# Reordering VectorE's work in the layer-1 attention: the residual update between the two halves of the softmax, and the mean square before the modulation

## The chip, the cores and the metric

The kernel runs on one core of a Trainium2 chip. The metric is the device time of one execution in microseconds (us). Most executions agree within about 0.3%. Everything is float32. The profile shown is of one execution, taken by the hardware profiler; times in it count from its first instruction.

Names of the engines: TensorE (PE, with its weight loads as PEld), VectorE (DVE), ScalarE (ACT), GpSimd (POOL), SyncE (SP). Each runs its own list of instructions strictly in the order in which it was written. They meet only at semaphores: an instruction waits until a counter has reached a number, and raises a counter when it is done.

## The reference, cut to what matters

128 sequences of 32 tokens with 128 features pass through two transformer blocks. Both are conditioned on one vector per sequence. The change is in the attention of the second one (layer 1), which has a single head of width 128:

```
x_in = x
h = rmsnorm(x, norm1_w) * (1 + scale) + shift          # scale, shift from cond
Q, K, V = h @ q_w + q_b, h @ k_w + k_b, h @ v_w + v_b
attn = softmax((Q @ K.T) * D ** -0.5, axis=-1)         # 32 keys for each token
x = x_in + (attn @ V) @ proj_w + proj_b
# behind it the second MLP:
x = x + gelu(film(rmsnorm(x, norm2_w)) @ mlp_w1 + mlp_b1) @ mlp_w2 + mlp_b2
```

## The kernel before, in words

The 4096 rows are 32 tiles of 128 rows (four sequences each), and four tiles are a group: there are 8 groups (`NG = 8`). All of `X` stays in SBUF. The kernel has four phases, each over all 8 groups: layer-0 attention, layer-0 MLP, layer-1 attention (`attention1`), layer-1 MLP (`mlp(3)`). A group's norm is prepared under a running number `gg = phase * 8 + g`, and this preparation runs ahead of the phase by two or three groups. There is no scheduler: every engine's order is written out by hand as a step function, and `group_steps` calls it for g = 0 to 7. Buffers are doubled; `p` is the half.

In step g of the layer-1 attention each engine does this, in this order:

- **TensorE**: `qkv1(g)`: Q and K into banks 2 and 3, then V (with the output projection already folded into its weights, `wvp`) into bank 4. The V part waits until VectorE has copied the previous group's V out of bank 4 (`v1_moved >= g`). Then `rows_T(g+2)` transposes the normed rows `xhat` of the group two ahead into `hT_ps` (bank 0); it waits for `xhat_ready`. Then `scores1(g)` into bank 7, which waits for ScalarE's copies of Q and K of this group. Then, for g of at least 2, `values1(g-2)`: attention weights `PT` times values `Vs`, into `y_ps` (bank 1). It waits for `pt1_ready`, `v1_moved` and for the update of group g-3, which empties the same bank.
- **ScalarE**: the exponential of group g-1 (`exps1`, `St<-Ss`), which waits for VectorE's subtraction of that group; two square sums of group g+3; the copies of Q and K of group g (`Qs`, `Kx`); two more square sums.
- **GpSimd**: `power1` (`rstd<-v_sb`) and `scale_rows` (`xhat<-X,rstd`) of group g+3, then `add_shift` (`h<-hA,B`) of group g+2, then `keep` (`xg<-X,row`, X plus the projection's bias) of group g.
- **VectorE**: `softmax1(g-1)`: row maximum and subtraction from bank 7 into `Ss`. `normalise1(g-1)`: the sum of the exponentials (`den`), its reciprocal (`rden`), the product `St<-St,rden`, and a transposition into `PT`. It waits for the exponential. `move_v1(g)` copies V from bank 4 to `Vs[p]`; that half of `Vs` is still read by `values1(g-2)`, so the copy waits for `y_ready`, which `values1(g-2)` raises. `modulate(g+2)` (`hA<-bank,A`). `mean_square(g+3)` (`v_sb<-ssq`), for which GpSimd's `power1` waits. `update(2, g-2)` (`X<-bank,xg`), which also needs the `y_ready` of `values1(g-2)`.

The lines which the prediction names: L539 and L541 maximum and subtraction; L547, L549, L551, L556 the four of `normalise1`; L563 V's copy; L481 `modulate`; L569 `mean_square`; L494 `update`; L388 and L381 GpSimd's `power1` and `scale_rows`; L332 `keep`; L308 `add_shift`; L879 the exponential; L895 and L897 the copies of Q and K; L887 the squares; L924 `rows_T`; L1094, L1095 and L1098 Q, K and V; L1108 `scores1`; L1121 `values1`; L949 the first matrix of the MLP (`up`); L1087 its second (`down`); L757 ScalarE's `xhat` of the MLP phase; L468 a part of VectorE's `aggregate`.

At the start of `mlp(3)` TensorE does `up` of group 0, chunks 0 and 1 (banks 2 and 3), `values1(6)`, chunks 2 and 3 (banks 4 and 5), `rows_T`, `values1(7)`; VectorE does `softmax1(7)`, `normalise1(7)`, `update(2,6)`, row statistics, `modulate`, `aggregate`.

Of the kernel before, what the change touches and what calls it, by code (L numbers as in the profile page):

```python
# [31 lines left out]
NG = NT // TG  # L32
# [26 lines left out]
def build(nc, x, cond, weights, columns, rows, out):  # L59
    with ExitStack() as ctx:  # L60
# [3 lines left out]
        def sem(name):  # L64
            return ctx.enter_context(nc.semaphore(name))
# [73 lines left out]
        qkv1_ready, qk1_moved, v1_moved, s1_ready, max1_ready, s1_used, p1_ready, den1_ready, rden1_ready, p1_scaled, pt1_ready, ssq_ready = (  # L139
            sem(n) for n in ("qkv1_ready", "qk1_moved", "v1_moved", "s1_ready", "max1_ready", "s1_used", "p1_ready", "den1_ready",  # L140
                             "rden1_ready", "p1_scaled", "pt1_ready", "ssq_ready"))
# [5 lines left out]
        def w(name, i=0, n=D):  # L147
            at = W_AT[name][0] + i * n
            return W[:, at:at + n]
# [8 lines left out]
        def by_tile(ap):  # L158
            return ap.rearrange("p (t d) -> p t d", t=TG)

        def by_seq(ap):
            return ap.rearrange("p (b t) -> p b t", t=L)

        def over_keys(ap):
            return ap.unsqueeze(2).broadcast_to([P, TG, L])

        def wait(eng, s, n):

            if not isinstance(n, int) or n > 0:
                eng.wait_ge(s, n)  # L170
# [11 lines left out]
        def known(g, low, high):  # L182

            return not isinstance(g, int) or low <= g < high

        def x_group(gg):

            if isinstance(gg, int):
                g = gg % NG
                return slice(g * TG, (g + 1) * TG)  # L190
            return bass.ds(((gg) % NG) * TG, TG)
# [236 lines left out]
        def _(dve):  # L428
# [46 lines left out]
            def modulate(gg, p, stats_of=None):  # L475

                if stats_of is not None:
                    dve.wait_ge(stats_done, stats_of + 1)
                dve.wait_ge(hT_ready, gg + 1)
                wait(dve, h_ready, gg - 1)  # L480
                dve.tensor_tensor(by_seq(hA[:, p, :]), by_seq(hT_ps[:, :]),  # L481
                                  A[:, seqs(gg)].unsqueeze(2).broadcast_to([P, GB, L]), ALU.mult).then_inc(hA_ready, 1)

            def update(phase, g, p):

                gg = phase * NG + g
                dve.wait_ge(y_ready, gg + 1)
                if phase < 2:
                    dve.wait_ge(x_updated, gg + 1)
                    dve.tensor_tensor(by_tile(yG[:, :]), by_tile(y_ps[:, :]), gate[:, phase, x_group(g), :],  # L490
                                      ALU.mult).then_inc(y_used, 1)
                else:
                    dve.wait_ge(xg_ready, gg + 1)
                    dve.tensor_tensor(X[:, x_group(g), :], by_tile(y_ps[:, :]), by_tile(xg[:, p, :]),  # L494
                                      ALU.add).then_inc(x_updated, 1)
# [40 lines left out]
            def softmax1(g, p):  # L536

                dve.wait_ge(s1_ready, g + 1)
                dve.tensor_reduce(max1[:, :], by_seq(bank[7][:, 0:P]), AX_X, ALU.max).then_inc(max1_ready, 1)  # L539
                dve.wait_ge(max1_ready, g + 1)  # L540
                dve.tensor_tensor(by_seq(Ss[:, p, 0:P]), by_seq(bank[7][:, 0:P]), over_keys(max1[:, :]),  # L541
                                  ALU.subtract).then_inc(s1_used, 1)

            def normalise1(g, p):

                dve.wait_ge(p1_ready, g + 1)
                dve.tensor_reduce(den1[:, :], by_seq(St[:, p, 0:P]), AX_X, ALU.add).then_inc(den1_ready, 1)  # L547
                dve.wait_ge(den1_ready, g + 1)
                dve.reciprocal(rden1[:, :], den1[:, :]).then_inc(rden1_ready, 1)  # L549
                dve.wait_ge(rden1_ready, g + 1)  # L550
                dve.tensor_tensor(by_seq(St[:, p, P:2 * P]), by_seq(St[:, p, 0:P]), over_keys(rden1[:, :]),  # L551
                                  ALU.mult).then_inc(p1_scaled, 1)
                dve.wait_ge(p1_scaled, g + 1)
                if known(g, 2, NG):
                    dve.wait_ge(y_ready, 2 * NG + g - 1)
                dve.transpose(PT[:, p, 0:P], St[:, p, P:2 * P]).then_inc(pt1_ready, 1)  # L556

            def move_v1(g, p):

                dve.wait_ge(qkv1_ready, 3 * g + 3)  # L560
                if known(g, 2, NG):
                    dve.wait_ge(y_ready, 2 * NG + g - 1)
                dve.tensor_copy(Vs[:, p, 0:GN], bank[4][:, :]).then_inc(v1_moved, 1)  # L563

            def mean_square(gg, p):

                dve.wait_ge(ssq_ready, gg - 2 * NG - 2)
                wait(dve, rstd_ready, gg - 1)
                dve.tensor_scalar(v_sb[:, p, :], ssq[:, p, :], 1.0 / D, 1e-6, ALU.mult, ALU.add).then_inc(v_ready, 1)  # L569
# [141 lines left out]
            def attention1(g, p):  # L711
                first = isinstance(g, int) and g == 0
                if not first:
                    softmax1(g - 1, 1 - p)
                    normalise1(g - 1, 1 - p)
                move_v1(g, p)
                if first:
                    mean_square(2 * NG + g + 3, 1 - p)
                    update(1, 7, 1)
                modulate(2 * NG + g + 2, p)  # L720
                if not first:
                    mean_square(2 * NG + g + 3, 1 - p)
                if known(g, 2, NG):
                    update(2, g - 2, p)

            group_steps(dve, attention0)
            group_steps(dve, mlp(1))
# [186 lines left out]
        def _(pe):  # L914
# [28 lines left out]
            def up(phase, g, p, chunks=range(NC)):  # L943

                m = (phase // 2) * NG + g
                pe.wait_ge(h_ready, phase * NG + g + 1)
                for n in chunks:
                    wait(pe, g_ready, NC * (m - 1) + n + 1)
                    last = pe.matmul(bank[2 + n][:, :], w(f"W1_{phase // 2}", n), h[:, p, :], start=True, stop=True)  # L949
                    last.then_inc(u_ready, 1)  # L950
# [46 lines left out]
            def output_T(g, p):  # L997

                pe.wait_ge(o_used, 2 * g + 2)
                pe.wait_ge(y_used, g + 1)  # L1000
                for t in range(TG):
                    last = pe.transpose(bank[1][:, P * t:P * (t + 1)], On[:, p, P * t:P * (t + 1)], ident[:, :])
                last.then_inc(ot_ready, 1)
# [108 lines left out]
            def wait_values1(g):  # L1112
                pe.wait_ge(pt1_ready, g + 1)
                pe.wait_ge(v1_moved, g + 1)
                pe.wait_ge(x_updated, 2 * NG + g + 1)

            def values1(p):
                for t in range(TG):
                    for b in range(TB):
                        rows_of = slice(L * b, L * (b + 1))  # L1120
                        last = pe.matmul(y_ps[rows_of, P * t:P * (t + 1)], PT[rows_of, p, L * t:L * (t + 1)],  # L1121
                                         Vs[rows_of, p, P * t:P * (t + 1)], start=True, stop=True)
                last.then_inc(y_ready, 1)

            def mlp(phase):
                def step(g, p):
                    gg = phase * NG + g
                    first = isinstance(g, int) and g == 0
                    if first and phase == 1:
                        output_T(7, 1)  # L1130
                    elif first:
                        up(phase, g, p, (0, 1))
                        wait_values1(6)
                        values1(0)
                        up(phase, g, p, (2, 3))
                    elif not (phase == 1 and isinstance(g, int) and g == 1):
                        up(phase, g, p)
                    if first and phase == 1:
                        up(1, 1, 1, (0, 1))
                        project0(7, 1)  # L1140
                        up(1, 1, 1, (2, 3))
                    if phase < 3 or not isinstance(g, int) or g < 6:
                        rows_T(gg + 2, p)
                    if not first:
                        down(phase, g - 1, 1 - p)
                    elif phase == 3:
                        wait_values1(7)
                        values1(1)
                return step
# [64 lines left out]
```

## Time and profile before

| | |
|---|---|
| time, median of 3 runs | 293.84 us (293.37 to 294.67) |
| the profiled execution's own time | 293.45 us |
| its span, first to last instruction | 291.6 us |
| mean granted TensorE clock | 0.988 of full speed |
| busy: PE, DVE, ACT, POOL | 251.1, 187.1, 165.3, 184.6 us |
| layer-1 attention, first Q matmul to last step's start of `mlp(3)` | about 177.4 to 226.3 us |

The span is 1.85 us shorter than the execution's own time. The busy times are sums over four phases with different limits, so what the change is worth has to be read in the layer-1 attention itself: about 49 us in which one step follows another at an even pace.

### The profile page before, as it was taken

What the parts mean: (1) busy time and instruction counts of PE and PEld (TensorE: products, weight loads), DVE (VectorE), ACT (ScalarE), POOL (GpSimd) and SP (SyncE); (2) the same over time, 40 slices, a digit from 0 to 9 for tenths busy, and PEclk for the clock granted to TensorE, in tenths of its full rate; (3) what the DMA queues carried; (4) which work ended last, traced back from release to release, by engine and by line L of the source; (5) the groups of instructions that cost most, each with busy time, mean ns of one, the idle gap of its engine ahead of it and who ended that gap; (6) DMA issues with size and microseconds to landing.
All of it is one profiled execution on the core that took longest, in us unless ns stands there. A gap on an engine that the chain in (4) does not pass through costs nothing.

```text
span 291.6 us, 8250 instructions
## 1 busy us (share of the span) xinstructions
PE 251.1 (86%) x2876; PEld 188.1 (64%) x2876; DVE 187.1 (64%) x535; ACT 165.3 (57%) x358; POOL 184.6 (63%) x187
## 2 busy tenths in 40 slices
PE   0687739797989979889999999987678989999996
PEld 0565529586787767567777778655455567777775
DVE  4898974988999989855455554665654855452002
ACT  2265755686797875785555556434554555555330
POOL 5645375647678677579787888676777654445310
PEclk9999996999999999999999999999999999999999
DMA  7952769424434338800000000000000001111112
GB/s 227 328 176 37 168 111 197 71 62 70 82 75 76 74 71 167 182 4 0 1 0 0 0 0 2 0 2 1 0 2 0 0 4 36 36 36 36 38 36 72
DMA packets 44569, 18.11 MB, mean 62 GB/s; under 512 B 32512, under 2 KB 43136, under 8 KB 44032
## 3 DMA queue, kind: packets, MB, share of 16 engines
q1 hardware_dynamic: 43968, 15.80, 24.6%
q10 hardware_dynamic: 576, 1.98, 2.0%
q8 instruction: 15, 0.25, 0.4%
q14 instruction: 10, 0.08, 0.1%
HBM read 11.35 MB, written 4.59 MB: 55 GB/s over the span
## 4 chain that ended last, share of the span: by engine, by line
PE 53%; DVE 12%; DMA 9%; ACT 9%; issue 8%; POOL 4%; SPq 1%; DVEq 1%; ACTq 1%; POOLq 0%
PE bank L1087 20%; PE bank L949 16%; PE bank L979 5%; DMA values_scratch<-Vs 5%; PE bank L924 4%; ACT Kx L772 4%; DMA Vx<-values_scratch 3%; PE bank L1121 3%; PE bank L992 2%; DMA X<-x 2%; DVE hA L481 2%; ACT xhat L757 2%; SPq L239 1%; PE bank L1008 1%; DVE X L494 1%
## 5 line engine op out<-in xcount | busy, mean ns | idle before, releaser
L757 ACT ACTIVATE xhat<-X,shift,rstd 128x128 f32 (+1 forms) x96 | 39.6, 486 | 53.3 <-POOL shift L297 53.1
L1087 PE MATMUL bank<-W,Qx 128*128 128x128 f32 x512 | 59.6, 275 | 0.0
L1087 PEld LDWEIGHTS bank<-W,Qx 128*128 128x128 f32 x512 | 58.5, 192 | 1.0 <-issue 1.0
L949 PE MATMUL bank<-h,W 128*128 128x512 f32 x128 | 58.6, 596 | 0.0
L308 POOL TENSOR_TENSOR h<-hA,B 128x512 f32<-128x512 f32 x32 | 33.9, 1060 | 23.1 <-DVE hA L481 22.8
L807 ACT ACTIVATE Qx<-bank,col 128x512 f32<-128x512 f32 x64 | 39.2, 679 | 8.6 <-PE bank L949 8.6
L481 DVE TENSOR_TENSOR hA<-bank,A 128x512 f32<-128x512 f32 x32 | 22.0, 689 | 32.7 <-PE bank L924 17.3
L979 PE MATMUL bank<-Kx,Qx 128*128 128x128 f32 x256 | 36.2, 286 | 4.6 <-DMA Qx<-Qs 1.6
L949 PEld LDWEIGHTS bank<-h,W 128*128 128x128 f32 x128 | 22.8, 190 | 22.4 <-issue 22.1
L979 PEld LDWEIGHTS bank<-Kx,Qx 128*128 128x128 f32 x256 | 31.8, 196 | 6.6 <-DMA Qx<-Qs 1.8
L339 POOL TENSOR_TENSOR X<-yG,xg 128x512 f32 (+1 forms) x16 | 20.4, 1275 | 18.6 <-DVE yG L490 18.5
L295 POOL TENSOR_TENSOR rstd<-v_sb,minus_half 128x4 f32<-128x4 f32 x24 | 24.5, 1019 | 11.2 <-DVE v_sb L472 6.7
L924 PE MATMUL bank<-ident,xhat 128*128 128x128 f32 x128 | 20.6, 284 | 12.3 <-POOL xhat L381 7.1
L924 PEld LDWEIGHTS bank<-ident,xhat 128*128 128x128 f32 x128 | 14.8, 143 | 22.6 <-issue 13.7
L772 ACT ACTIVATE Kx<-bank,k_bias,r_mask 128x512 f32<-128x512 f32 x32 | 23.1, 777 | 9.7 <-PE bank L960 9.7
L315 POOL TENSOR_TENSOR Ss<-Sc,smax 128x512 f32<-128x512 f32 x16 | 16.8, 1049 | 17.7 <-DVE smax L505 17.6
L992 PEld LDWEIGHTS bank<-Vx,PT 128*32 128x32 f32 x1024 | 11.4, 112 | 21.9 <-issue 12.6
L332 POOL TENSOR_TENSOR xg<-X,row 128x512 f32<-128x512 f32 x16 | 20.3, 1269 | 7.1 <-DVE X L494 7.0
L789 ACT ACTIVATE PT<-St 128x512 f32<-128x512 f32 x32 | 20.3, 635 | 7.5 <-DVE St L518 7.5
L494 DVE TENSOR_TENSOR X<-bank,xg 128x512 f32 (+1 forms) x15 | 10.3, 686 | 19.8 <-PE bank L1087 19.8
L518 DVE STREAM_TRANSPOSE St<-Ss 128x512 f32<-128x512 f32 x32 | 21.9, 683 | 1.0 <-POOL Ss L315 0.9
L452 DVE BATCH_NORM_STATS2 stats<-X 128x6 f32 (+1 forms) x96 | 20.6, 278 | 2.7 <-DMA X<-x 2.2
(123 smaller groups left out, 414.9 us busy)
## 6 DMA issues: line engine op xcount, KB each, us to landing
values_scratch<-Vs SPq DMA_DIRECT2D x8, 288.0 KB, 2.5
Vx<-values_scratch SPq DMA_DIRECT2D x32, 72.0 KB, 2.6
gate<-gates_scratch SPq DMA_DIRECT2D x8, 256.0 KB, 4.8
gate<-gates_scratch SPq DMA_DIRECT2D x4, 512.0 KB, 7.6
Qx<-Qs SPq DMA_DIRECT2D x28, 64.0 KB, 2.3
out<-X SPq DMA_DIRECT2D x7, 256.0 KB, 2.3
W<-weights ACTq DMA_DIRECT2D x1, 1152.0 KB, 6.8
X<-x SPq DMA_DIRECT2D x4, 256.0 KB, 7.0
```

Of the source, the lines that this page charges most:

```text
L295: pool.tensor_tensor(rstd[:, p, :], v_sb[:, p, :], minus_half[:, :], ALU.pow).then_inc(pool_chain, 1)
L308: pool.tensor_tensor(by_seq(h[:, p, :]), by_seq(hA[:, p, :]), B[:, seqs(gg)].unsqueeze(2).broadcast_to([P, GB, L]), ALU.add).then_inc(h_re ...
L452: last = dve.bn_stats(stats[:, t, :], X[:, x_tile(gg, t), :])
L481: dve.tensor_tensor(by_seq(hA[:, p, :]), by_seq(hT_ps[:, :]), A[:, seqs(gg)].unsqueeze(2).broadcast_to([P, GB, L]), ALU.mult).then_inc(hA_ ...
L518: dve.transpose(St[:, t % 2, :], Ss[:, t % 2, :]).then_inc(st_ready, 1)
L757: last = act.activation(xhat[:, p, P * t:P * (t + 1)], X[:, x_tile(gg, t), :], ACT.Identity, bias=shift[:, p, t:t + 1], scale=rstd[:, p, t ...
L772: last = act.activation(Kx[:, p, q, :], bank[3][:, :], ACT.Identity, bias=k_bias[:, q:q + 1], scale=r_mask[:, q:q + 1])
L807: act.activation(gT[:, p, n, :], bank[2 + n][:, :], ACT.Gelu, bias=bias).then_inc(g_ready, 1)
L924: last = pe.transpose(hT_ps[:, P * t:P * (t + 1)], xhat[:, p, P * t:P * (t + 1)], ident[:, :])
L949: last = pe.matmul(bank[2 + n][:, :], w(f"W1_{phase // 2}", n), h[:, p, :], start=True, stop=True)
L979: last = pe.matmul(bank[4 + t % 2][:, P * b:P * (b + 1)], Qx[:, p, TB * t + b, :, :].rearrange("p a t -> p (a t)"), Kx[:, p, :, at:at + L] ...
L1087: last = pe.matmul(y[t // 2][:, P * t:P * (t + 1)], gT[:, p, n, P * t:P * (t + 1)], w(f"W2_{phase // 2}", n), start=(n == 0), stop=(n == N ...
```

## The change

VectorE's step of the layer-1 attention gets another order. Before: maximum and subtraction of g-1; the rest of the softmax of g-1; V's copy of g; modulation of g+2; mean square of g+3; update of g-2. After: maximum and subtraction of g-1; update of g-2; the rest of the softmax of g-1; V's copy of g; mean square of g+3; modulation of g+2. In step 0 nothing changes (V's copy, mean square, update of the layer-0 MLP's last group, modulation). In step 1 there is no update, and only the mean square and the modulation change places. No instruction on VectorE is added or removed.

On TensorE one wait is added: before the first `up` of the layer-1 MLP it waits until V of all 8 groups has been copied (`v1_moved >= 8`). Before, the wait for the update of group 5 ahead of `values1(6)` covered this, because the update stood behind V's copy in VectorE's order.

```diff
@@ VectorE, attention1(g, p) @@
                 first = isinstance(g, int) and g == 0
                 if not first:
                     softmax1(g - 1, 1 - p)
+                if known(g, 2, NG):
+                    update(2, g - 2, p)
+                if not first:
                     normalise1(g - 1, 1 - p)
                 move_v1(g, p)
+                mean_square(2 * NG + g + 3, 1 - p)
                 if first:
-                    mean_square(2 * NG + g + 3, 1 - p)
                     update(1, 7, 1)
                 modulate(2 * NG + g + 2, p)
-                if not first:
-                    mean_square(2 * NG + g + 3, 1 - p)
-                if known(g, 2, NG):
-                    update(2, g - 2, p)
@@ TensorE, mlp(phase) @@
                     if first and phase == 1:
                         output_T(7, 1)
                     elif first:
+                        pe.wait_ge(v1_moved, NG)
                         up(phase, g, p, (0, 1))
                         wait_values1(6)
                         values1(0)
```

## Rows read from the trace of the kernel before

**Rows 1.** The page, its first line.

```profile
span 291.6 us, 8250 instructions
```

**Rows 2.** Busy time by engine of one step (start:end, length, then each engine's).

```profile
201.20:207.50 6.30, 4.97 (x81) 3.35 (x82) 3.82 (x11) 2.74 (x11) 4.34 (x4) 1.00 0.00 0
```

**Rows 3.** Chain of waits that ended last, two pieces of one step (start, length).

```profile
208.86 0.59 DVE X L494
...
211.56 0.68 ACT Kx L897
```

**Rows 4.** Timeline of one step: start, length, engine, line, [idle before <- releaser].

```profile
207.49 0.69 DVE L563 COPY Vs<-bank 128x512 f32<-128x512 f32 x1 [1.84 <-PE bank L1121]
208.10 0.68 DVE L481 TENSOR_TENSOR hA<-bank,A 128x512 f32<-128x512 f32 x1
...
208.70 0.16 DVE L569 TENSOR_SCALAR v_sb<-ssq 128x4 f32<-128x4 f32 x1
...
208.77 0.68 DVE L494 TENSOR_TENSOR X<-bank,xg 128x512 f32 x1
208.94 1.02 POOL L388 TENSOR_TENSOR rstd<-v_sb,minus_half 128x4 f32<-128x4 f32 x1 [1.59 <-DVE v_sb L569]
...
209.68 0.29 DVE L541 TENSOR_TENSOR Ss<-bank,max 128x128 f32<-128x128 f32 x1
...
210.08 0.31 ACT L879 ACTIVATE St<-Ss 128x128 f32<-128x128 f32 x1 [3.59 <-DVE Ss L541]
...
211.28 0.65 PE L924 MATMUL bank<-ident,xhat 128*128 128x128 f32 x4 [1.05 <-POOL xhat L381]
...
212.24 1.26 POOL L332 TENSOR_TENSOR xg<-X,row 128x512 f32<-128x512 f32 x1
...
212.28 0.46 PE L1108 MATMUL bank<-Kx,Qs 128*32 128x32 f32 x32 [0.35 <-ACT Kx L897]
...
213.82 0.69 DVE L563 COPY Vs<-bank 128x512 f32<-128x512 f32 x1 [2.10 <-PE bank L1121]
```

**Rows 5.** Timeline of VectorE, the rest of the softmax of group 7.

```profile
229.25 0.29 DVE L547 TENSOR_REDUCE den<-St 128x4 f32<-128x128 f32 x1 [0.38 <-ACT St L879]
229.57 0.18 DVE L549 RECIPROCAL rden<-den 128x4 f32<-128x4 f32 x1
229.79 0.33 DVE L551 TENSOR_TENSOR St<-St,rden 128x128 f32<-128x128 f32 x1
230.16 0.31 DVE L556 STREAM_TRANSPOSE PT<-St 128x128 f32<-128x128 f32 x1
230.39 0.65 DVE L494 TENSOR_TENSOR X<-bank,xg 128x512 f32<-128x512 f32 x1
```

**Rows 6.** Timeline of step 1 to 2, VectorE beside GpSimd.

```profile
189.31 0.90 DVE L569 TENSOR_SCALAR v_sb<-ssq 128x4 f32<-128x4 f32 x1
...
191.63 1.04 POOL L381 TENSOR_TENSOR xhat<-X,rstd 128x512 f32<-128x512 f32 x1 [0.24 <-POOL rstd L388]
191.64 1.18 DVE L551 TENSOR_TENSOR St<-St,rden 128x128 f32<-128x128 f32 x1
```

**Rows 7.** Timeline, V's copies of step 2 and step 7 (the first and last of six).

```profile
194.91 0.69 DVE L563 COPY Vs<-bank 128x512 f32<-128x512 f32 x1 [1.66 <-PE bank L1121]
...
226.39 0.69 DVE L563 COPY Vs<-bank 128x512 f32<-128x512 f32 x1 [2.10 <-PE bank L1121]
```

**Rows 8.** Timeline of TensorE at the start of the layer-1 MLP.

```profile
226.26 1.99 PE L949 MATMUL bank<-h,W 128*128 128x512 f32 x4
...
228.50 1.08 PE L1121 MATMUL bank<-Vs,PT 32*32 32x128 f32 x32 [0.26 <-DVE X L494]
...
237.32 0.65 PE L924 MATMUL bank<-ident,xhat 128*128 128x128 f32 x4 [0.76 <-ACT xhat L757]
```

**Rows 9.** TensorE's clock: timeline, one window (clock third from last), longest waits after 51 us.

```profile
43.32 0.71 PE L992 MATMUL bank<-Vx,PT 128*32 128x36 f32 x32 [3.90 <-DMA Vx<-values_scratch]
...
42.00:43.00 1.00, 0.00 (x0) 0.00 (x0) 0.95 (x3) 0.00 (x0) 1.00 (x2) 0.71 0.73 116
...
PE bank L992 <- DMA Vx<-values_scratch: 3.8, 4, 1.6
```

## The prediction

> **What bounds the kernel now.** I read the page first: the span is 291.6 us [rows 1], and the profiled execution took 293.45 us, so 1.85 us lie around the span. That execution is 0.39 us under the median of the runs, 293.84 us. TensorE is the busiest engine, but the question is the layer-1 attention alone. So I read a table of busy time by stretch there: in one step of 6.30 us TensorE has 4.97 us of work, GpSimd 4.34, VectorE 3.82, ScalarE 2.74 [rows 2]. No engine is full. The pace must come from a loop through several of them.
>
> The chain of waits names the loop. In every step it goes through VectorE's update and through ScalarE's copy of K [rows 3]. The timeline of one step gives its lengths [rows 4]. I measure from the moment at which `values1` is seen to be done, which is the start of V's copy (207.49):
>
> - V's copy to modulation 0.61, to mean square 0.60, to update 0.07, to subtraction 0.91 (209.68, with the maximum in between), to the exponential 0.40 (210.08). Sum 2.59.
> - From the exponential to the scores, through squares, Q's copy and K's copy: 212.28 less 210.08, 2.20. TensorE stood idle for the last 0.35 of it because of K's copy.
> - From the scores to the next V copy, through `values1`: 213.82 less 212.28, 1.54.
>
> 2.59 + 2.20 + 1.54 = 6.33, one step. Over five steps the V copies go from 194.91 to 226.39 [rows 7], which is 6.30 each. A second loop is almost as long: mean square (208.70), GpSimd's power and `xhat`, the transposition of rows at 211.28, 2.58 later. TensorE waited 1.05 for it, but the scores behind it waited another 0.35 for K's copy. So the second loop has 0.35 us to spare.
>
> The reader should see what is **not** in the loop: the rest of the softmax. Its four instructions run while `values1` is still to come, and then VectorE stands idle for 1.84 to 2.10 us before V's copy [rows 4]. Today that part costs nothing, and this idle time is its cover.
>
> **The change part by part.**
>
> *Update before the rest of the softmax.* The update of g-2 needs `values1(g-2)`, the last thing in TensorE's step g. VectorE executes in order, so everything behind the update now starts after `values1` is done: the rest of the softmax, V's copy, mean square, modulation and, in the next step, the maximum and the subtraction for which the exponential waits. The cover is gone. The idle time moves ahead of the update, where nothing fills it. The price is what lies between the start of the sum `den` and the instruction behind the transposition. Row by row it is 0.32 + 0.22 + 0.37 + 0.23: 230.39 less 229.25 is 1.14 [rows 5]. The other members of the chain are the same as before in another order, so they add nothing. The new first loop is 6.30 + 1.13 = 7.43: I start from the mean step and take 1.13, since the product's own length varies by some hundredths.
>
> *Mean square before modulation.* This takes 0.60 out of the second loop, but the update (0.60) and the rest of the softmax (1.14) come in ahead of the mean square, where V's copy (0.61) stays and the modulation (0.60) leaves. Mean square starts at 0.60 + 1.14 + 0.60 = 2.34 after `values1`, where it was at 1.21. The rows' transposition starts 2.58 later, at 4.92, and ends at 5.57. The scores can go when K's copy is there: at 2.59 + 1.14 + 2.20 = 5.93. So the first loop stays in front, by 0.36, and the move is worth nothing. Below nothing is excluded for a reason: no instruction of the first loop goes away.
>
> *V's copy* comes at 1.74 and ends at 2.43 (0.69 long). TensorE's V matmuls for the next group need bank 4. They come after Q and K, which take about 2.1, so they start some 0.3 late. That is inside the time in which TensorE waits for `xhat` anyway (until 4.92), and costs nothing.
>
> *How often.* The update stands in steps 2 to 7. The loop is closed from step 2's `values1` to step 7's: five turns, 5 x 1.13 = 5.65. Step 1 has only the exchange of mean square and modulation. There the mean square took 0.90 instead of 0.16 [rows 6], so moving it ahead may give or cost some tenths; I take a gain of 0.1.
>
> *The start of the MLP.* Before, TensorE began `up` at 226.26, or 0.13 before V's copy of step 7, and then idled 0.26 until the update of group 5 let `values1(6)` go [rows 8]. Now it waits for V's copy of step 7, which ends at 2.43, so `up` starts at about 2.5, 2.63 later than before. The 0.26 of idle time falls away because the update is long done. Net 2.63 - 0.26 = 2.37. Nothing later gives it back: the next wait of TensorE, 0.76 at 237.32 for ScalarE's `xhat` [rows 8], follows from the rows' transposition that stands behind these same matmuls, and so moves with them. The bounds here are 0.9 (were the copy seen 1.14 earlier and hidden partly behind the exponential) and 3.0.
>
> *The product beside GpSimd.* It was 0.33 in one row and 1.18 in another, which began 0.01 after GpSimd's `xhat` and ended just behind it [rows 5, 6]. These are the two bounds of this instruction. In the new order GpSimd's step ends with `keep` (212.24 to 213.50), 0.3 before the next `values1` is seen, and GpSimd then waits for a mean square that comes at 2.34. The product runs at about 1.15 to 1.5. So I take 0.33. The Trainium skill has a rule for this, in "SBUF — State Buffer", section "SBUF: two separate sides": VectorE with two SBUF inputs and GpSimd share a port pair that one of them locks for a whole instruction. By that rule too the product is free here, since GpSimd is idle; the sum by the rule is the same unless GpSimd runs late, which is a rival below.
>
> **Sum**: 5.65 - 0.1 + 2.37 = 7.92. 293.45 + 7.9 = 301.4 for a profiled execution, and 293.84 + 7.9 = **301.7** for the median. This is 2.7% slower. What a measurement of this kernel can tell from no change is about 0.5%, or 1.5 us.
>
> **Rivals.**
>
> 1. *The rest of the softmax stays hidden* (not slower). If it did not delay the subtraction, the first loop would remain 6.33, and the second would be 0.60 + 0.60 + 2.58, then 0.65 for the rows, then 1.54: 5.97, shorter. Only the MLP's start would pay: V's copy ends at 1.29, `up` starts 1.5 later than before, less 0.26: +1.2, or 295.0, within 0.5%. For it speaks that exponentials are ready early in the new order, so `den` itself waits for nobody. Against it: it decides itself by whether `values1(g-2)` is done when VectorE reaches the update, and VectorE reaches it after the subtraction, at some 3.7 in a step of 7.4. It would have to be 3.7 us earlier. 3%.
> 2. *A collision with GpSimd in every step.* `keep` ends only about 0.3 before the update starts. If GpSimd's instructions move by more than 1.2 us against VectorE's, the product is blocked and takes up to 1.18: 0.85 more in each of five steps, 4.2, so 306. Against it: GpSimd's 4.34 of work fits into 7.4. 5%.
> 3. *TensorE's clock falls.* It was granted half speed (1.2 of 2.4 GHz) for some microseconds after TensorE had been idle for 3.90 us; within that idle time the clock went to 0.71 for the window 42 to 43. Later waits of up to 1.6 us left it at full speed [rows 9]. Now TensorE idles up to 1.3 us in a step, and about 2.5 at the start of the MLP, between the two. One step at half speed would be 2 x 4.97 = 9.9 of TensorE's work [rows 2] instead of a step of 7.4: 2.5 more, 304.2. 8%.
> 4. *A smaller price*: the MLP absorbs part of its late start (0.9 instead of 2.37), giving 300.2. 10%.
> 5. *It turns out faster* by something I don't see, such as the early update freeing `y_ps`: nobody waits for that bank within the phase. At best 0.35 of loop slack times five, 292.1. 3%.
>
> **How the numbers follow.** The forecast has 71%, with 300.6 to 302.8 of its own. The range 299.6 to 304.6 takes in rivals 4 and 3; outside are 1, 2 and 5 and the rest. Slower by over 0.5%: forecast, 2, 3 and 4, 94%. Within 0.5%: 3%. Faster: 3%.
>
> **What would show it.** In the profile after: V's copies of steps 2 to 7 some 7.4 us apart, with no idle time before them. VectorE's long idle time stands before the update instead, ended by `values1`, and is about 3.8 us (a step of 7.43, less 3.33 to the subtraction and its own 0.29). `den` has no wait for the exponential. TensorE waits some 1.3 for `xhat` and 0.3 for K's copy in each step. `up` starts behind V's copy with about 2.5 us of idle time. It would be wrong if the steps were still 6.3 apart (rival 1), if the product took over 1 us (rival 2), or if the clock in the stage were below 1 (rival 3).

## The result and the profile after

The changed kernel took 305.23 us (median of 4 runs, 303.55 to 306.81), the kernel before 294.25 us (4 runs). The ratio is 1.0365, with a 95% interval of 1.0317 to 1.0413. The forecast was 301.7 us with a range of 299.6 to 304.6. The direction was right and the added time was 11 us instead of 7.9, outside the range.

The page after, its span and the granted clock of TensorE in 40 slices (tenths of full speed; each slice is 7.6 us):

```profile
span 303.8 us, 8256 instructions
...
PEclk9999988799999999999999999997899799999999
```

The clock now falls twice more, in slices 28 and 29 and in slice 32 (counted from 1), which is the layer-1 attention and the start of the MLP behind it. Before, it stayed at full speed from 51 us on.

The timeline of one step in which the clock was at 1, the columns as in [rows 4]:

```profile
195.21 0.69 DVE L494 TENSOR_TENSOR X<-bank,xg 128x512 f32 x1 [4.71 <-POOL xg L332]
...
195.81 0.28 DVE L547 TENSOR_REDUCE den<-St 128x4 f32<-128x128 f32 x1
...
196.12 0.18 DVE L549 RECIPROCAL rden<-den 128x4 f32<-128x4 f32 x1
...
196.34 0.29 DVE L551 TENSOR_TENSOR St<-St,rden 128x128 f32<-128x128 f32 x1
...
196.99 0.65 DVE L563 COPY Vs<-bank 128x512 f32<-128x512 f32 x1
...
197.56 0.15 DVE L569 TENSOR_SCALAR v_sb<-ssq 128x4 f32<-128x4 f32 x1
197.62 0.68 DVE L481 TENSOR_TENSOR hA<-bank,A 128x512 f32<-128x512 f32 x1
197.69 1.16 PE L1097 MATMUL bank<-wvp,h 128*128 128x128 f32 x8 [0.77 <-DVE Vs L563]
...
198.53 0.29 DVE L541 TENSOR_TENSOR Ss<-bank,max 128x128 f32<-128x128 f32 x1
...
198.94 0.31 ACT L878 ACTIVATE St<-Ss 128x128 f32<-128x128 f32 x1 [5.67 <-DVE Ss L541]
...
200.14 0.66 PE L923 MATMUL bank<-ident,xhat 128*128 128x128 f32 x4 [1.29 <-POOL xhat L381]
...
201.14 0.46 PE L1107 MATMUL bank<-Kx,Qs 128*32 128x32 f32 x32 [0.34 <-ACT Kx L896]
...
202.81 0.69 DVE L494 TENSOR_TENSOR X<-bank,xg 128x512 f32 x1 [3.98 <-PE bank L1120]
```

The reader should see here what [rows 4] had hidden: VectorE idles ahead of the update, 3.98 us until `values1` is done, and `den` with the rest of the softmax runs behind it without any wait for the exponential. (For the first update shown, GpSimd's `xg` is named as the releaser: it ended at 195.05, `values1` at 195.01, so the two came together there. From the next update on only `values1` is late.) From update to update it is 7.60 us, in the terms of the forecast: from there to the exponential 3.73 (forecast 2.59 + 1.14), to the scores 2.20 (as before), to the next update 1.67. Only the last one is new: it was 1.54 when V's copy was the first instruction behind `values1`. TensorE waits 1.29 for `xhat` and 0.34 for K's copy, nearly as forecast. The product is 0.29: GpSimd was idle beside it.

The next step looks different. Again the timeline, of TensorE alone:

```profile
205.20 1.16 PE L1097 MATMUL bank<-wvp,h 128*128 128x128 f32 x8 [0.69 <-DVE Vs L563]
207.82 1.08 PE L923 MATMUL bank<-ident,xhat 128*128 128x128 f32 x4 [1.46 <-POOL xhat L381]
208.83 0.66 PE L1107 MATMUL bank<-Kx,Qs 128*32 128x32 f32 x32
209.42 1.93 PE L1120 MATMUL bank<-Vs,PT 32*32 32x128 f32 x32
```

and the busy time in stretches of 2 us there (columns as in [rows 2], TensorE's the first behind the length, granted clock third from last):

```profile
204.00:206.00 2.00, 1.31 (x9) 0.80 (x8) 1.97 (x6) 0.00 (x0) 0.62 (x1) 1.00 0.00 0
206.00:208.00 2.00, 0.55 (x5) 0.36 (x4) 0.30 (x2) 1.63 (x7) 1.75 (x3) 0.97 0.00 0
208.00:210.00 2.00, 2.00 (x48) 1.56 (x51) 0.00 (x0) 1.10 (x5) 1.92 (x2) 0.50 0.00 0
210.00:212.00 2.00, 2.00 (x30) 1.29 (x23) 0.46 (x1) 0.00 (x0) 0.00 (x0) 0.68 0.00 0
```

The same 32 matmuls of `values1` took 1.93 instead of 1.08, at 0.50 of full speed (1.2 of 2.4 GHz), in a place where everything waits for them. The update came at 211.54, so this step was 8.73 us long. In the stretches ahead of the fall TensorE had been busy 1.31 and 0.55 of 2 us. The same happens at the start of the MLP, behind the wait that the change added:

```profile
237.17 2.41 PE L948 MATMUL bank<-h,W 128*128 128x512 f32 x4 [2.60 <-DVE Vs L563]
...
239.51 1.93 PE L1120 MATMUL bank<-Vs,PT 32*32 32x128 f32 x32
```

**Where the time went.** The place at which the layer-1 attention is reached varies from execution to execution by up to 4 us, whatever the kernel (182.8 to 186.7 in the profiles here). So I measure from the last gated update of the layer-0 MLP (`yG<-bank,gate`, L490) to the end of the span, and cut it at the first instruction behind `values1`, in step 2 and in step 7. Every number is a difference of two starts in a timeline, or of a start and the span:

| kernel | L490 to step 2 | steps 2 to 7 (five) | step 7 to the end | sum |
|---|---|---|---|---|
| before | 11.16 | 31.48 | 65.21 | 107.85 |
| changed | 11.06 | 39.57 | 69.02 | 119.65 |
| changed, again | 11.06 | 39.78 | 69.09 | 119.93 |
| forecast for changed | 11.06 | 37.13 | 67.58 | 115.77 |

The excess over the forecast, 3.88 us, is 2.44 in the steps and 1.44 behind them. Both parts contain matmuls at half clock. What else is in them has to come from the experiments.

### The profile page after: what moved, and what is told of

The parts are those of the page before. It is cut to its first block, busy times and chain, and to the rows that moved or that the text cites. A ratio compares the mean times of both kernels' runs of the same rounds, so it can differ in the third digit from the quotient of the medians.

```text
span 303.8 us, 8256 instructions
## 1 busy us (share of the span) xinstructions
PE 256.8 (85%) x2876; PEld 190.6 (63%) x2876; DVE 183.5 (60%) x535; ACT 165.0 (54%) x358; POOL 184.2 (61%) x187
## 3 DMA queue, kind: packets, MB, share of 16 engines
q10 hardware_dynamic: 576, 1.98, 2.0%
## 4 chain that ended last, share of the span: by engine, by line
PE 54%; DVE 13%; DMA 9%; issue 8%; ACT 7%; POOL 4%; SPq 3%; DVEq 1%; ACTq 1%; POOLq 0%
PE bank L1086 19%; PE bank L948 16%; PE bank L978 5%; DMA values_scratch<-Vs 4%; PE bank L923 4%; DMA Vx<-values_scratch 3%; PE bank L1120 3%; ACT Kx L771 2%; PE bank L991 2%; DMA X<-x 2%; ACT xhat L756 1%; DVE X L494 1%; DVE hA L481 1%; SPq L239 1%; PE bank L1007 1%
## 5 line engine op out<-in xcount | busy, mean ns | idle before, releaser
L948 PE MATMUL bank<-h,W 128*128 128x512 f32 x128 | 59.3, 602 | 2.6 <-DVE Vs L563 2.6
```

## The experiments

Times are medians of the runs of each kernel; ratios are against the kernel before on the same chip, with 95% intervals. Executions of one kernel spread more than the 0.3% named at the start: those of the kernel before went from 292.3 to 297.0 us. In the last group of four one execution of the kernel before took 870 us and one of the run `e11` 901 us; I can't explain them, and they move the medians by 0.13 us at most. The orders in the diffs are those of VectorE's step in the layer-1 attention for g of at least 1.

### The update alone, and the exchange alone

```diff
 # e1_update_only, against the changed kernel
                 move_v1(g, p)
-                mean_square(2 * NG + g + 3, 1 - p)
                 modulate(2 * NG + g + 2, p)
+                mean_square(2 * NG + g + 3, 1 - p)
 # e2_mean_square_only, against the kernel before
-                modulate(2 * NG + g + 2, p)
                 mean_square(2 * NG + g + 3, 1 - p)
+                modulate(2 * NG + g + 2, p)
```

> The update stands between the two halves of the softmax as in the change, but the modulation still stands ahead of the mean square (order: maximum and subtraction, update, rest of the softmax, V's copy, modulation, mean square). My theory (the update before the rest of the softmax carries the whole price, steps of 7.6 us, and half a clock for part of the stage) says 305 to 307 us: the loop through mean square and GpSimd gets 0.6 us longer, of which 0.36 was spare, so 0.1 to 0.25 per step over the changed kernel's 7.6. The rival that the exchange of mean square and modulation costs the time says about 294.

> The kernel before with only mean square and modulation exchanged, the update last. My theory says no change, 294 us (293.5 to 294.8) with steps of 6.3, since the loop through mean square already had 0.35 us to spare and the other loop keeps all its members. The rival that the exchange has a price says over 296, the rival that it is a gain hidden inside the change says under 293.

Measured: 306.89 us (305.21 to 310.0; ratio 1.0411, 1.0344 to 1.0478) for the update alone (with the wait that it needs on TensorE), 293.95 us (ratio 0.9998, 0.9971 to 1.0025) for the exchange alone, where V's copies stay 6.25 and 6.32 apart. The whole loss comes with the update and its wait, and the exchange by itself is worth nothing, as its 0.35 us of spare time in [rows 4] said. The profile of the first was its slowest execution; in it three steps of 9.3 us alternate with two of 7.9, and the clock in the slow ones is well below 1 (here 218 to 226 against 226 to 234):

```profile
218.00:226.00 8.00, 7.70 (x80) 4.82 (x80) 3.39 (x10) 1.59 (x7) 3.23 (x4) 0.60 0.00 0
226.00:234.00 8.00, 5.12 (x80) 3.22 (x80) 3.39 (x10) 2.72 (x12) 4.43 (x5) 1.00 0.00 0
```

The 7.9 is more than the 7.4 to 7.6 of the changed kernel's steps at full clock: once the update stands early, the loop through the mean square is the longer one unless the mean square goes first, so inside the change the exchange saves some 0.3 per step.

### The rest of the softmax back under its cover

```diff
                 softmax1(g - 1, 1 - p)
+                normalise1(g - 1, 1 - p)
                 if known(g, 2, NG):
                     update(2, g - 2, p)
-                normalise1(g - 1, 1 - p)
                 move_v1(g, p)
```

> The changed kernel with the update moved behind the rest of the softmax but still ahead of V's copy (and with the added wait on TensorE). If the loss comes from the rest of the softmax standing behind the wait for values1, it is hidden again: steps of 6.4 to 6.5 (0.14 over before, because the update seems to start 0.14 later after values1 than V's copy did), the start of the MLP 1.3 late, the clock at 1 in the stage, 296.3 us (295.3 to 297.3). If any move of the update ahead of V's copy costs the full price: 303 to 305.

Measured: 295.74 us (294.06 to 296.95), ratio 1.0052 (1.0024 to 1.008). The timeline of VectorE, two updates one step apart:

```profile
203.11 0.69 DVE L494 TENSOR_TENSOR X<-bank,xg 128x512 f32 x1 [2.23 <-PE bank L1122]
203.71 0.68 DVE L563 COPY Vs<-bank 128x512 f32<-128x512 f32 x1
...
209.47 0.69 DVE L494 TENSOR_TENSOR X<-bank,xg 128x512 f32 x1 [1.96 <-PE bank L1122]
```

The update is still ahead of V's copy, and the step is 6.42 on average. So it is not the early update that costs the time but what stands behind it: putting the four instructions of the rest of the softmax back in front gives back 1.1 of the 1.2 that each step had grown by at full clock (below), and the clock stays at 1 in the stage. This also settles the "not slower" rival: it would have been right if the rest had stayed hidden, and it did not stay hidden.

### TensorE's added wait, later

```diff
                     elif first:
-                        pe.wait_ge(v1_moved, NG)
                         up(phase, g, p, (0, 1))
                         wait_values1(6)
                         values1(0)
+                        pe.wait_ge(v1_moved, NG)
                         up(phase, g, p, (2, 3))
```

> The changed kernel with TensorE's added wait placed behind values1(6), ahead of the chunks that write bank 4, so that the first two chunks of the MLP start without it. My theory gives back the 2.4 us of the late start, and up to 1.5 more if the slow clock behind that idle time goes too: 300.5 to 303 us, or 2.2 to 4.5 under the changed kernel's 305. If the late start was absorbed by the MLP in the changed kernel: no difference, 305.

Measured: 301.3 us (300.53 to 303.79), ratio 1.0268 (1.0209 to 1.0328): 3.9 us under the changed kernel's 305.23. The part from step 7 to the end is 66.10 instead of 69.02, so the place of this wait costs 2.9 in the profiles, the slow matmuls behind it included; against the 67.40 that this part takes with the wait in its place and the clock at 1 (e5, below) it is 1.30. It does not come down to the 65.21 of before: `values1(7)` now waits 0.51 for an update, and TensorE's wait for ScalarE's `xhat` behind it is 1.25 instead of the 0.76 of [rows 8].

```profile
234.42 1.07 PE L1120 MATMUL bank<-Vs,PT 32*32 32x128 f32 x32
235.43 1.98 PE L948 MATMUL bank<-h,W 128*128 128x512 f32 x4
237.28 0.66 PE L923 MATMUL bank<-ident,xhat 128*128 128x128 f32 x4
238.45 1.08 PE L1120 MATMUL bank<-Vs,PT 32*32 32x128 f32 x32 [0.51 <-DVE X L494]
```

Four `up` matmuls take 1.98 and `values1` 1.07 and 1.08: no half clock here. (In the steps the clock did fall once: one of the five is 8.47.)

### Is it the clock? The idle time filled

The next kernels add matmuls from constant operands into a free PSUM bank; nobody reads the results.

```diff
+            def fill(n):
+                for _ in range(n):
+                    pe.matmul(bank[6][:, 0:P], w("W1_1", 0, D), w("W1_1", 1, D), start=True, stop=True)
...
+                if known(g, 2, NG):
+                    fill(2)
                 wait(pe, v1_moved, g)
...
+                if known(g, 2, NG):
+                    fill(4)
                 rows_T(2 * NG + g + 2, p)
...
+                        fill(8)          # e5 only
                         pe.wait_ge(v1_moved, NG)
```

> The changed kernel again, beside the next three on the same chip: 305 us (303.5 to 307), with the clock below 1 in some stretches of the layer-1 attention.

> The changed kernel with matmuls added in TensorE's idle time, whose results nobody reads: two of 128x128x128 ahead of the V matmuls and four ahead of the rows' transposition in steps 2 to 7, eight ahead of the added wait at the MLP's start. They fit in the idle time (0.26 us each; gaps of 0.77, 1.3 and 2.6). If the granted clock falls because TensorE idles, it stays at 1 and the time drops although work was added: 302 to 303.3 us, every step 7.6, the clock's mean at 0.985 or more. If the long steps have another cause, or the added work is on the path, 305 or more.

> As the one with all the added matmuls, but without the eight at the MLP's start. The clock theory: steps stay at 7.6 with clock 1, but the 2.6 us of idle time ahead of the MLP is followed by slow matmuls, so 0.5 to 1.5 us over the run with all of them: 303 to 304.5. If that idle time alone does not bring the clock down: the same as with all of them.

Measured on one chip: the changed kernel again 304.65 us (303.64 to 304.92; ratio 1.0368, 1.0293 to 1.0444), with all the added matmuls 302.5 us (301.86 to 303.16; ratio 1.0311, 1.0238 to 1.0385). The two ratios' intervals overlap, but all four executions with the added work are faster than all four without. TensorE's mean granted clock agrees: 0.983 to 0.994 in the four filled executions, 0.960 to 0.976 in seven of the eight of the changed kernel (one had 0.989, and still took 303.64 us). The profile is clearer. The page's clock after 68 us holds no slice below 9, and a stretch of the steps with the timeline of TensorE in it reads:

```profile
202.00:210.00 8.00, 7.09 (x109) 5.08 (x98) 3.40 (x11) 2.73 (x11) 4.38 (x5) 1.00 0.00 0
```

```profile
205.97 1.06 PE L1093 MATMUL bank<-W 128*128 128x128 f32 x8
207.59 0.66 PE L923 MATMUL bank<-ident,xhat 128*128 128x128 f32 x4 [0.56 <-POOL xhat L381]
208.34 0.46 PE L1114 MATMUL bank<-Kx,Qs 128*32 128x32 f32 x32
208.73 1.08 PE L1127 MATMUL bank<-Vs,PT 32*32 32x128 f32 x32
```

`values1` is back at 1.08, and all five steps are 7.41 to 7.60. This gives the change's price without the clock: 37.62 for the five steps and 67.40 behind them, against 39.57 and 69.02. Less work on TensorE was slower than more. The same holds over all profiles of kernels with the early update and the long step: the clock fell in the steps of all five without added matmuls there (both of the changed kernel, e1, e4, e7) and of none of the three with them (e5, e6, e11). The added matmuls themselves cost 0.52 in step 2, which had no idle time for them (L490 to step 2 is 11.58 instead of 11.06). The medians support a smaller price than the profiles: 304.65 - 302.5 = 2.15, or some 2.7 with these 0.52 added.

Without the eight at the MLP's start the times were 301.67 us (301.01 to 305.87, 5 runs; ratio 1.0262, 1.0189 to 1.0334), not the 303 to 304.5 that was expected. Its profile, the slowest of the five, has 69.07 behind step 7, 1.67 more than with the eight, and the clock there is 0.52 from 238 to 240: it did fall behind the 2.6 us of idle time. So it did in all four profiles with this wait (the changed kernel's two, e1 and this one, 69.02 to 69.10). But three of its five executions took 301.01 to 301.67 us, less than the 303 or so that the earliest arrival of any profile (L490 at 182.76), this profile's 118.29 us behind it and the 1.9 around the span would give (an estimate). That points to executions in which it did not fall. How often it does is open.

### The same matmuls where there is nothing to gain

> Control for the added matmuls: the kernel before with four of 128x128x128 (1.05 us) ahead of the rows' transposition in steps 2 to 7, in idle time of 1.05 to 1.2, results read by nobody. The clock is at 1 in that stage anyway, so there is nothing to gain: 294 us, within 0.5% of before. If the added matmuls themselves made a stage faster in another way, under 292.5.

This is the kernel before with `fill(4)` ahead of `rows_T` in steps 2 to 7. Measured: 294.28 us (292.6 to 295.15), ratio 0.9977 (0.9944 to 1.001); the steps are 6.24 to 6.32. These four matmuls per step speed nothing up by themselves where the clock is at 1 (the two ahead of V's matmuls and the eight of the MLP's start were not in this control).

### V's copy first behind the wait

```diff
                 softmax1(g - 1, 1 - p)
+                move_v1(g, p)
                 if known(g, 2, NG):
                     update(2, g - 2, p)
                 normalise1(g - 1, 1 - p)
-                move_v1(g, p)
                 mean_square(2 * NG + g + 3, 1 - p)
 # e11_copy_first_filled: also fill(6) ahead of rows_T in steps 2 to 7
```

> The changed kernel with V's copy as the first instruction behind values1 (order: maximum and subtraction, V's copy, update, rest of the softmax, mean square, modulation). The same instructions stand behind the wait, so my theory keeps the loop; if the update as first one starts 0.14 us later than V's copy would, undisturbed steps are 7.45 instead of 7.59. TensorE's V matmuls and the MLP's start come 1.7 us earlier, which takes the late start away and part of the idle time: 300 to 302.5 us. If the order behind the wait did not matter to the MLP's start, 305.

> The order with V's copy first behind values1 (then update, rest of the softmax, mean square, modulation), with six matmuls of 128x128x128 ahead of the rows' transposition in steps 2 to 7, results read by nobody. TensorE idles 2.3 there, so they fit. The clock theory: no step above 7.75, the steps still 7.5 to 7.7, and with the MLP's start not late 299.5 to 301 us, against 304.1 without them. If its long steps were not the clock's: 303 or more.

Measured: 304.1 us (302.36 to 306.22; ratio 1.0376, 1.0281 to 1.0471), and 303.04 us with the added matmuls (ratio 1.0259, 1.0196 to 1.0323). Both medians are above what was expected, and 303 or more was set down as the sign that the long steps are not the clock's. By its time alone `e11` thus speaks against the clock; its profile does not. Two things show in the profiles. The steps did not become shorter: with the clock at 1 they are 7.50 and 7.72 in turn, mean 7.63, where the changed kernel with the filled idle time has 7.52. The timeline of one such step, mean square and modulation of VectorE, the rows' transposition, the scores, the next V copy, and mean square and modulation again:

```profile
221.01 0.13 DVE L569 TENSOR_SCALAR v_sb<-ssq 128x4 f32<-128x4 f32 x1
221.24 0.69 DVE L481 TENSOR_TENSOR hA<-bank,A 128x512 f32<-128x512 f32 x1
...
223.73 0.65 PE L925 MATMUL bank<-ident,xhat 128*128 128x128 f32 x4 [2.27 <-POOL xhat L381]
...
224.69 0.46 PE L1109 MATMUL bank<-Kx,Qs 128*32 128x32 f32 x32 [0.31 <-ACT Kx L898]
...
226.22 0.69 DVE L563 COPY Vs<-bank 128x512 f32<-128x512 f32 x1 [3.77 <-PE bank L1122]
...
228.60 0.14 DVE L569 TENSOR_SCALAR v_sb<-ssq 128x4 f32<-128x4 f32 x1
228.88 0.69 DVE L481 TENSOR_TENSOR hA<-bank,A 128x512 f32<-128x512 f32 x1
```

From the scores to the first instruction behind `values1` it is 1.53 again, so V's copy does start 0.14 earlier than the update. But from the mean square to the modulation it is 0.23 and, in the next step, 0.28, where it was 0.06 in the changed kernel, and that eats the gain and a little more. Why it is longer here no run shows. The expectation counted the first and not the second. And the profiled execution with the added matmuls reached the stage 4.0 us later than the one without (L490 at 186.72 against 182.76). From L490 on, the added matmuls gain what the clock theory says: steps 38.16 instead of 39.78, none above 7.72. The part behind step 7 is 67.07 instead of the changed kernel's 69.02, but most of that is the clock, which stayed at 1 there: against the 67.40 at full clock it is 0.33. In e7 TensorE waits 0.81 instead of 2.60 for V's copy, and loses most of the difference again in later waits, 0.77 for an update and 1.24 for ScalarE's `xhat`.

### The other way: work out from behind the wait

```diff
 # e8_modulate_early, against the kernel before, g of at least 1
                 softmax1(g - 1, 1 - p)
                 normalise1(g - 1, 1 - p)
+                modulate(2 * NG + g + 2, p)
                 move_v1(g, p)
-                modulate(2 * NG + g + 2, p)
                 mean_square(2 * NG + g + 3, 1 - p)
                 update(2, g - 2, p)
 # e9_softmax_early, g of at least 1 (step 0 ends with softmax1(0, 0))
-                softmax1(g - 1, 1 - p)
                 normalise1(g - 1, 1 - p)
                 modulate(2 * NG + g + 2, p)
+                softmax1(g, p)
                 move_v1(g, p)
                 mean_square(2 * NG + g + 3, 1 - p)
                 update(2, g - 2, p)
 # ScalarE, sum_squares
-                    act.wait_ge(v_ready, gg - 1)
+                    act.wait_ge(v_ready, gg)
```

> The opposite of the change: work is moved out from behind the wait for values1 into VectorE's idle time ahead of it. Order in step g: maximum and subtraction, rest of the softmax, modulation, V's copy, mean square, update. The modulation needs only the rows' transposition, which is over when values1 starts. If the step is the loop through what VectorE does behind values1, it loses the modulation's 0.60: steps of 5.7 instead of 6.3, 291 us (290.3 to 292). If something else sets the step of the kernel before (K's copy itself, TensorE), steps stay over 6.1 and the time within 0.5% of before.

> One step further: maximum and subtraction of group g, which need only the scores of g, also stand ahead of V's copy. Order in step g: rest of the softmax of g-1, modulation, maximum and subtraction of g, V's copy, mean square, update. ScalarE's wait ahead of the squares is for the mean square of one group later. The loop through the exponential is opened; what remains is V's copy, mean square, GpSimd, transposition, scores, values1: 0.61 + 2.58 + 0.65 + 1.54 = 5.4. By my theory 289.7 us (288.8 to 291). If ScalarE's or TensorE's own work sets the pace by then, no gain over the run with only the modulation moved.

Measured: 290.73 us (290.5 to 292.06; ratio 0.9871, 0.982 to 0.9922) and 289.29 us (288.55 to 293.55; ratio 0.9802, 0.9745 to 0.9859), both where expected. V's copies are 5.65 and 5.72 apart in the first. In the second they are 5.31 to 5.53 apart, and the timeline shows the maximum and the subtraction beside `values1`, ahead of V's copy, and what is left of VectorE's idle time:

```profile
206.41 0.69 DVE L481 TENSOR_TENSOR hA<-bank,A 128x512 f32<-128x512 f32 x1 [1.74 <-POOL h L308]
206.54 1.08 PE L1122 MATMUL bank<-Vs,PT 32*32 32x128 f32 x32
207.02 0.28 DVE L539 TENSOR_REDUCE max<-bank 128x4 f32<-128x128 f32 x1
207.33 0.29 DVE L541 TENSOR_TENSOR Ss<-bank,max 128x128 f32<-128x128 f32 x1
...
207.68 0.69 DVE L563 COPY Vs<-bank 128x512 f32<-128x512 f32 x1
...
208.29 0.16 DVE L569 TENSOR_SCALAR v_sb<-ssq 128x4 f32<-128x4 f32 x1
208.35 0.68 DVE L494 TENSOR_TENSOR X<-bank,xg 128x512 f32 x1
```

The second version beats both kernels of the case, by 2.0% (interval 1.4 to 2.6) and by more than 5%. The loop of the forecast thus held in both directions.

All profiles from L490 on, in one table (parts as above):

| kernel | to step 2 | five steps | step 7 to the end | sum |
|---|---|---|---|---|
| e1, update only | 11.30 | 43.65 | 69.10 | 124.05 |
| e2, exchange only | 10.93 | 31.46 | 65.43 | 107.82 |
| e3, whole softmax first | 11.05 | 32.11 | 66.34 | 109.50 |
| e4, wait later | 11.06 | 38.68 | 66.10 | 115.84 |
| e5, all filled | 11.58 | 37.62 | 67.40 | 116.60 |
| e6, steps filled | 11.58 | 37.64 | 69.07 | 118.29 |
| e7, copy first | 11.39 | 39.78 | 67.07 | 118.24 |
| e11, copy first, filled | 11.44 | 38.16 | 67.08 | 116.68 |
| e8, modulation early | 11.15 | 28.47 | 64.85 | 104.47 |
| e9, softmax early | 11.52 | 26.94 | 64.93 | 103.39 |
| e10, before, filled | 11.15 | 31.45 | 65.24 | 107.84 |

## Why the prediction was right and where it failed

- **What bounds the stage**: right. The pace was set by the loop through what VectorE does behind `values1`. Lengthening that list by 1.14 lengthened the step by 1.2, shortening it by 0.60 shortened it by 0.6 (e8).
- **Update before the rest of the softmax**: mechanism right, size a little low. The term was 5 x 1.13 = 5.65; at full clock it measures 37.62 - 31.48 = 6.14 (e5), or 1.23 per step. What was missing is the 0.13 by which the update starts later behind `values1` than V's copy had (1.67 instead of 1.54 from the scores). The list from the update to the exponential is 3.73, as forecast, in one step and 3.56 in the next; before, it was 2.59 and 2.51 in turn, so it grew by 1.10 on average.
- **Mean square before modulation, V's copy, the product beside GpSimd**: right for the loop. The exchange alone is worth nothing (e2), V's matmuls ran 0.77 late inside time that TensorE waits anyway (forecast 0.3), and the product took 0.29 with GpSimd idle beside it, so rival 2 did not come. That V's late matmuls cost nothing holds for the loop only: their wait is one of those ahead of the clock's fall.
- **The start of the MLP**: right at full clock. Forecast 2.37, measured 67.40 - 65.21 = 2.19. TensorE's next wait for ScalarE's `xhat` was 0.75 there, as before, so nothing absorbed the late start, and rival 4's smaller price did not come. Its lower bound of 0.9 does not follow from the 1.14 given with it, which makes 1.23. The wait's place is only part of the 2.19: with the wait later (e4) 1.30 of it goes, and 0.89 stays with the new order.
- **The clock**: here the prediction failed. It was rival 3, with a chance of 8% and a price of 2.5. The step that failed is the comparison by the longest single idle time: TensorE had idled 3.90 us before its clock fell [rows 9], single waits up to 1.6 had left it at full speed, so the new waits of 1.3 were taken as harmless, only the one of 2.5 as doubtful, and the sum had no term for the clock. In the changed kernel the clock fell with no single wait above 1.5 nearby: several short waits stood close together (0.69, then 1.46), and TensorE's unchanged work stood in a longer step: about 5 us of 7.5 instead of 4.97 of 6.30. That work, 4.97 us, was in my rows; I used it for the price and not for the chance. That the sum of the waits decides is argued, not shown: no run separates it from other reasons, and the same waits left the clock at 1 in some steps (1.29 in the changed kernel's first step, 2.27 in a step of e7). The rival's price was low too: it counted one step at half clock, 304.2 us, and the profile has three slow places, the steps of 8.73 and 8.22 and the MLP's start. In the profile the clock costs 39.57 - 37.62 = 1.95 in the steps and 69.02 - 67.40 = 1.62 behind them, 3.6 of the 3.9 us by which the forecast was too low; in the medians it is some 2.7 of 3.5, and what the rest is stays open. The filled kernel shows that it is the clock, and e10 that the filling is not a gain of its own. The start of the MLP, where a 2.60 us wait stood, is the place that the prediction had doubted; the steps are the one it had not.

The sum by the measured terms: -0.1 + 6.14 + 2.19 + 3.57 = 11.80, which is 119.65 - 107.85. The -0.1 for step 1 was a guess between some tenths either way; that it came out at 11.06 - 11.16 is luck.

## What to carry to other kernels

On an engine that executes in order, an instruction's price is set by which side of a late wait it stands on: list what is behind the wait that closes the loop, and move out everything that does not need it (here the modulation, then the maximum and the subtraction, for 2%). A step that gets longer while TensorE's work stays the same leaves TensorE idle for longer in sum; look at all its waits there and not only at the longest, which did not foretell the fall here, because the clock can fall and lengthen just the matmuls on the loop. To find out whether a loss is the clock's, fill the idle time with matmuls that nobody reads, and run the same filling in the kernel before as a control.

## What the runs showed of the hardware

In the changed kernel's steps the granted clock fell to 0.50 (1.2 GHz) behind short waits, none above 1.5 us. The five steps (columns as in [rows 2]):

```profile
195.20:202.80 7.60, 5.20 (x81) 3.22 (x81) 3.39 (x10) 2.73 (x11) 4.30 (x4) 1.00 0.00 1
202.80:211.50 8.70, 6.56 (x81) 4.16 (x81) 3.39 (x10) 2.73 (x11) 4.29 (x4) 0.80 0.00 0
211.50:219.80 8.30, 5.92 (x81) 3.75 (x81) 3.43 (x11) 2.72 (x11) 4.30 (x4) 0.90 0.01 2
219.80:227.20 7.40, 5.89 (x81) 3.68 (x81) 3.37 (x11) 2.73 (x11) 4.29 (x4) 0.88 0.00 0
227.20:234.80 7.60, 4.99 (x80) 2.94 (x79) 3.40 (x11) 2.72 (x11) 4.29 (x4) 1.00 0.00 0
```

The 6.56 of the slowest step is the same 81 matmuls, part of them at half clock. The clock was not below 1 in every step, and the steps were 7.60, 8.73, 8.22, 7.43 and 7.59 long. The Trainium skill, "TensorE: Matmul & The Clock Gate", section "Why this matters for your kernels", asks for no long idle gap between bursts of matmuls; to keep to that was not enough here, where the clock fell in the steps although every gap was short. And a low clock costs only where matmuls are on the loop: `values1` at 1.93 instead of 1.08 lengthened its step, while in the fourth step, at a mean of 0.88, the slow matmuls were mainly Q's at its start (2.08 instead of 1.12), ahead of a wait of 1.40 for `xhat`, and the step took 7.43, as long as at full clock (7.41 and 7.42 in e5).
